# Last batch of expert units: the second-layer weights by plain SyncE transfers, the second bias by VectorE, and another order at the hand-over

## The reference, cut to what matters

```python
idx = jnp.argmax(probs, axis=-1)
pos = (jnp.cumsum(one_hot, axis=0) * one_hot).sum(-1).astype(jnp.int32) - 1
kept = pos < C
buf = jnp.zeros((E, C, D), dtype=h.dtype).at[idx, pos_safe].set(x, mode='drop')
hmid = jax.nn.relu(jnp.einsum('ecd,edf->ecf', buf, w1) + b1[:, None, :])
ybuf = jnp.einsum('ecf,efd->ecd', hmid, w2) + b2[:, None, :]
y_tok = ybuf[idx, pos_g] * (prb * kept)[:, None]
```

## Time and profile before

| | |
|---|---|
| median of 3 runs | 2496.98 us (2493.55 to 2497.48) |
| profiled execution, its own time | 2497.35 us |
| its span, first to last instruction | 2495.6 us |
| PE / DVE / ACT / POOL busy | 82% / 61% / 41% / 74% |
| mean granted TensorE clock | 0.930 of full speed |
| PE busy from 2320 to 2340 us | 20.00 of 20 us |
| second-bias products L1279 | 105, 22 of them in the last batch |

### The profile page before, as it was taken

The page is one execution under the profiler, slowest core; times in us unless marked ns, Lnnn a source line. Parts: engine busy times, 40 slices in busy tenths (PEclk is TensorE's granted clock), DMA queues, the critical chain, the costliest instruction groups (busy, mean ns, idle before and its releaser), DMA issues. The chain is left out here.

```text
span 2495.6 us, 42607 instructions
## 1 busy us (share of the span) xinstructions
PE 2049.6 (82%) x12873; PEld 1578.1 (63%) x12873; DVE 1511.6 (61%) x5293; ACT 1033.6 (41%) x2479; POOL 1849.9 (74%) x1924
## 2 busy tenths in 40 slices
PE   0048999994677787998989989998989998787997
PEld 0015666662455565776768777776778777676986
DVE  6776555554358777787747556566565666565332
ACT  4663333331244444543434433443444444352332
POOL 7777777777777777777777777777777777765575
PEclk9999999996788887999999999999998999898999
DMA  9846666664566667777777777777887888778653
GB/s 337 321 138 178 174 175 175 175 172 128 150 195 201 194 190 255 237 238 222 244 232 227 248 231 234 233 229 253 304 295 273 306 304 293 249 274 305 239 180 108
DMA packets 279195, 568.84 MB, mean 228 GB/s; under 512 B 51493, under 2 KB 180142, under 8 KB 259791
## 3 DMA queue, kind: packets, MB, share of 16 engines
q0 software_dynamic: 98352, 268.90, 35.3%
q1 hardware_dynamic: 150225, 245.97, 28.9%
q10 hardware_dynamic: 30390, 51.21, 5.6%
HBM read 506.09 MB, written 87.86 MB: 238 GB/s over the span
## 5 line engine op out<-in xcount | busy, mean ns | idle before, releaser
L967 POOL DMA_INDIRECT rows_sb<-xn_scratch,src_sb x1517 | 1458.3, 961 | 462.2 <-issue 456.7
L1261 PE MATMUL bank<-acc 128*128 128x128 f32 (+1 forms) x2624 | 434.4, 319 | 3.6 <-ACT acc L2042 2.9
L1285 PE MATMUL bank<-acc 128*128 128x256 f32 x1680 | 413.1, 390 | 0.0
L1261 PEld LDWEIGHTS bank<-acc 128*128 128x128 f32 x2624 | 379.2, 202 | 27.3 <-issue 5.6
L1079 PE MATMUL bank<-rows_sb,s_sb 128*24 128x256 f32 x3082 | 229.7, 419 | 198.6 <-DMA rows_sb<-xn_scratch,src_sb 198.0
L2059 ACT ACTIVATE acc<-bank,acc 128x128 f32<-128x128 f32 (+1 forms) x656 | 211.9, 398 | 368.5 <-PE bank L1261 368.2
L1285 PEld LDWEIGHTS bank<-acc 128*128 128x128 f32 x1680 | 313.9, 194 | 48.8 <-issue 0.4
L1549 DVE TENSOR_TENSOR acc<-acc,bank 128x48 f32 x831 | 170.5, 205 | 264.8 <-PE bank L1089 150.2
L1079 PEld LDWEIGHTS bank<-rows_sb,s_sb 128*24 128x24 f32 x3082 | 85.5, 108 | 272.8 <-issue 240.4
L1976 ACT COPY sums<-bank 120x256 f32<-120x256 f32 x208 | 76.5, 368 | 355.6 <-PE bank L1079 355.5
L2007 ACT ACT_TABLE_LOAD x95 | 121.9, 1283 | 200.8 <-PE bank L1168 199.9
(11 more groups left out here) (277 smaller groups left out, 3633.7 us busy)
## 6 DMA issues: line engine op xcount, KB each, us to landing
acc<-ffn_first_in SPq DMA_DIRECT2D x64, 1028.0 KB
acc<-ffn_w_in SPq DMA_DIRECT2D x64, 1024.0 KB
arena<-xn_scratch SPq DMA_DIRECT2D x194, 128.0 KB, 3.1
h_scratch<-arena ACTq DMA_DIRECT2D x97, 256.0 KB
rows_sb<-xn_scratch,src_sb POOLq DMA_INDIRECT x1517
xnt_scratch<-arena SPq DMA_DIRECT2D x97, 128.0 KB, 2.3
arena<-xnt_scratch SPq DMA_DIRECT2D x97, 128.0 KB
arena<-x_in SPq DMA_DIRECT2D x97, 128.0 KB
```

The lines of the kernel that those rows point to most:

```text
L967: pool.indirect_dma_start(out=chunk_row(c), out_offset=None, in_=xn_d, in_offset=bass.IndirectOffsetOnAxis(ap=src_sb[:, c:c + 1], axis=0)) ...
L1261: m = pe.matmul(bank[:, i * tokens:(i + 1) * tokens], w1_sb[k % 2][:, h, f * P:(f + 1) * P], xt[:, k % 2, h, 0:tokens], start=h == 0, stop ...
L1285: m = pe.matmul(bank[:, i * D:(i + 1) * D], hid[:, f, i * P:(i + 1) * P], w2_sb[k % 2][:, f, :], start=False, stop=f == FC - 1 and i == 0)
```

## The change

- GpSimd's `load_new_second` goes. SyncE loads the second-layer weights of all 22 units of the last batch in full, whether the expert is a new one or not. The first-layer loads stay as they are.
- For the last batch TensorE's bias product, its mask and the wait for it go. SyncE loads the unit's bias row to all partitions (`load_bias`, 128 KB), behind the second-layer loads of a place, and VectorE's `finish_unit` does one operation more, (bias x probability) + y.
- The last batch's order changes. `wanted_at` is one place later, so that unit 60's tokens are turned at the head of tick (60, 1), place 220, and no longer in tick (59, 2), place 219; by the planner's arithmetic no other tick, gather or load moves. At place 216 TensorE does the `sums` products before the two ticks (58, 1) and (58, 2), which stood on either side of them. VectorE reads `sums` at once, queues the units after four of the seven tables, and does the unit finishes of places 215 to 217 (units 56 and 57) only after the slots are filled. Their scatters move to place 218, behind the gathers of units 60 and 61.

```diff
+        b2_sb = [rows_sb[:, ROW_SLOTS - 2 + i, :] for i in range(2)]
...
+        HELD = range(chosen_at[-1], last_c + 1)
...
-        wanted_at = [slots_at[b] + (4 if slots_at[b] + 4 < PAIRS else 2) for b in batch_of]
+        wanted_at = [slots_at[b] + (4 if slots_at[b] + 4 < PAIRS else 2 if slots_at[b] < PAIRS else 3) for b in batch_of]
...
-            if e_place[n] == sums_at[-1] and ("unit", n - 1) not in here:
-                here.insert(0, ("unit", n))
-            elif e_place[n] >= PAIRS or ("unit", n - 1) in here or after == len(here):
+            if e_place[n] >= PAIRS or ("unit", n - 1) in here or after == len(here):
                 here.append(("unit", n))
...
+            if k in FINAL:
+                b2_at[max([known] + [done_place(k - 2) + 1] * (k - 2 in FINAL))].append(k)
...
-            scatter_at[min(done_place(k) + 1, PLACES - 1)].append(k)
+            scatter_at[last_c + 1 if done_place(k) in HELD else min(done_place(k) + 1, PLACES - 1)].append(k)
...
+            def load_bias(k):
+                x_ = expert_of(k)
+                sp.wait_ge(pair_mm, PAIRS)
+                if k - 2 in FINAL:
+                    sp.wait_ge(y_done, k - 1)
+                sp.dma_start(b2_sb[k % 2], ffn_b2[bass.ds(x_, 1), :].broadcast_to([P, D])
+                             ).then_inc(b2_ld[k % 2], 16)
...
                 for k in w2_at[p]:
-                    if k not in SKIPS:
-                        load_second(k)
+                    load_second(k)
                 for k in keep_at[p]:
                     keep_unit(k)
+                for k in b2_at[p]:
+                    load_bias(k)
...
-                for k in w2_at[p]:
-                    if k in SKIPS:
-                        load_new_second(k)
...
-                    if k in SKIPS:
-                        pe.wait_ge(new2_ld[k % 2], new_value(k))
-                    else:
-                        pe.wait_ge(w2_ld[k % 2], w2_value(k))
-                    pe.wait_ge(hot_spread, k + 1)
+                    pe.wait_ge(w2_ld[k % 2], w2_value(k))
+                    if k not in FINAL:
+                        pe.wait_ge(hot_spread, k + 1)
...
-                    for i, col in enumerate(columns_of(k)):
+                    for i in range(size(k) if k not in FINAL else 0):
                         pe.matmul(bank[:, i * D:(i + 1) * D], hot_wide.bitcast(F32R), b2_parts.bitcast(F32R),
                                   start=i == 0, stop=False)
...
+                    if k == sums_at[-1]:
+                        for n, at in enumerate(e_place):
+                            if at == k:
+                                unit_tick(n)
                     read_small(k, False)
                 elif kind == "end":
-                    read_small(k, True)
+                    if k != rank_at[-1]:
+                        read_small(k, True)
...
                             build_table(t)
+                            if t == routes[-1][RT - 1]:
+                                read_small(k, True)
...
-                if k < K and j == 1:
+                if k < FINAL[0] and j == 1:
...
+                    if k in FINAL:
+                        dve.wait_ge(b2_ld[k % 2], b2_value(k))
+                        link(dve.scalar_tensor_tensor(y[:, 0, :], b2_sb[k % 2], sprb[:, columns_of(k)[0]:columns_of(k)[0] + 1],
+                                                      y[:, 0, :], ALU.mult, ALU.add))
...
-                for kind, k in side[p]:
-                    if kind == "unit" and p >= PAIRS:
-                        finish_unit(k)
+                if p >= PAIRS and p not in HELD or p == last_c:
+                    for n, at in enumerate(e_place):
+                        if at == p or p == last_c and at in HELD:
+                            finish_unit(n)
```

More of the change, by code:

```diff
@@ L314, in build @@
         zero_st, far_kept, acc_ld = sem("zero_st"), sem("far_kept"), sems("acc_ld", 4)
-        new1_ld, new2_ld, rows_known = sems("new_w1_ld", 2), sems("new_w2_ld", 2), sem("rows_known")
+        new1_ld, b2_ld, rows_known = sems("new_w1_ld", 2), sems("b2_ld", 2), sem("rows_known")
         dve_seq, act_seq = sem("dve_seq"), sem("act_seq")
@@ L554, in build @@
         sums_at = [p + 1 for p in chosen_at]
+        HELD = range(chosen_at[-1], last_c + 1)
+        assert HELD[0] > PAIRS and rank_at[-1] == sums_at[-1] == build_at[-1]
         def most_ticks(p):
@@ L607, in done_place @@
             return e_place[last_tick[k] + FLUSH]
-        w1_at, w2_at, gather_at, scatter_at = ([[] for _ in range(PLACES)] for _ in range(4))
+        w1_at, w2_at, b2_at, gather_at, scatter_at = ([[] for _ in range(PLACES)] for _ in range(5))
+        assert all(size(k) == 1 for k in FINAL)
         for k in range(K):
@@ L614, in build @@
             w2_at[max([known] + [place_of(k - 1, 2)] * (k > 1))].append(k)
+            if k in FINAL:
+                b2_at[max([known] + [done_place(k - 2) + 1] * (k - 2 in FINAL))].append(k)
             lag = wanted_at[k] - slots_at[batch_of[k]] - 1
             ahead = 1 if turn_place[k] < PAIRS + 2 else 3
-            asked = max(known - 1 + lag, turn_place[k] - ahead)
+            asked = max(known - 1 + lag if slots_at[batch_of[k]] < PAIRS else known, turn_place[k] - ahead)
             if wanted_at[k] >= PAIRS:
@@ L652, in new_value, with b2_value @@
             return 16 * ((k - SKIPS[0]) // 2 + 1)
+        def b2_value(k):
+            return 16 * ((k - FINAL[0]) // 2 + 1)
         def w2_value(k):
@@ L1020, in load_new_first @@
                     bounds_check=NE * P - 1, oob_is_err=False).then_inc(new1_ld[k % 2], 16)
[L1022 to L1028, removed]
             for p in range(PLACES):
@@ L1285, in second_layer @@
                         m = pe.matmul(bank[:, i * D:(i + 1) * D], hid[:, f, i * P:(i + 1) * P], w2_sb[k % 2][:, f, :],
-                                      start=False, stop=f == FC - 1 and i == 0)
+                                      start=k in FINAL and f == 0 and i == 0, stop=f == FC - 1 and i == 0)
                 m.then_inc(l2_mm, 1)
@@ L1791, in side_step @@
                             build_table(t)
+                            if t == routes[-1][RT - 1]:
+                                read_small(k, True)
                 elif kind == "unit":
-                    unit_tick(k)
+                    if e_place[k] != sums_at[-1]:
+                        unit_tick(k)
                     if e_place[k] < PAIRS:
```

## The result

The changed kernel takes 2507.11 us (median of 6 runs, 2504.58 to 2511.04) against 2497.68 us (6 runs, 2493.55 to 2499.53): a ratio of 1.0034, 95% interval [1.0023, 1.0045]. It is 0.34% slower; the forecast was 2497.6 us, with a range to 2503.5. The profiled executions differ by 9.0 us in span (2504.6 against 2495.6).

The account below looks back on a forecast made before the run. The prediction took TensorE to bound the tail (busy 20.00 of 20 us). Its terms, -6.8 - 2.7 + 0.5 - 1.5 + 11.1, gave +0.6 us: 2497.6 us against the median, overall range 2487 to 2503.5.

Parts of the forecast that it names:

- SyncE's queue: Last batch: second-layer loads behind load-backs come late, stalling units 67 and 71 by 5.4 us each, unit 75 by 0.3: +11.1 us.
- T: The end of unit 65's first layer, from which the forecast counted load 67's times; units 71 and 75 are counted likewise.
- Unit 75: Its second-layer load stands behind load-back 9, of half the size, with no real first-layer load beside it: 0.3 us.
- Bias products: TensorE in the last batch: 22 products of 0.31 us leave the path, units 7.44 us apart: -6.8 us.
- GpSimd's loads: Tail: five issues a unit instead of six let GpSimd keep pace, so TensorE's stalls go: -2.7 us.
- The hand-over: Before unit 60: earlier table reading and new order gain, partly lost waiting for unit 59's mask: -1.5 us.
- VectorE's added operation: Counts only behind the last unit, between ScalarE's scaling and the last scatter: +0.5 us.
- Added traffic: Twelve formerly skipped 1.05 MB loads and 22 of 128 KB: nothing, up to +3 us in the first six units.
- The queue costs more: Rival: load 67 lands last, unit 75 loses 2 us too, 2503 us; chance 0.20, shared with an unseen added stall.

Follow-up runs that it names:

- the kernel with the order alone: The kernel before with only the new hand-over order, bias products and second-layer loads as before: 2496.39 us, ratio 0.9985 to the kernel before.
- the kernel with both mends: The changed kernel with weight loads ahead of the load-back in SyncE's queue and unit 59's mask ahead of units 56 and 57's finishes: 2486.43 us.
- the run without it: The changed kernel with the second-layer loads of units 64 to 81 given back to GpSimd: 2500.56 us, ratio 1.0000 to the kernel before.
- The run with the mask first: The changed kernel with VectorE writing unit 59's mask ahead of the finishes of units 56 and 57: 2506.06 us, ratio 1.0026 to the kernel before.
- the kernel with all mends: The changed kernel with weight loads before load-backs, unit 59's mask before the finishes, same-expert second-layer loads skipped, and small load-backs whose buffers are already free: 2478.89 us.
- the kernel with the loads first: The changed kernel with weight loads ahead of the load-back within each place of SyncE's queue: 2489.76 us, ratio 0.9962 to the kernel before.

## Why the prediction was wrong

Step by step, by its own terms; sizes are those of the profiled execution.

- **SyncE's queue, forecast +11.1 us: this is the step that failed.** Place, order and releaser were right: load-back 7 goes out at T + 8.84 us (forecast T + 8.65; T is 2346.50), load 67 at T + 10.03 (T + 9.75), and TensorE waits, then works at the low clock. The size was wrong, in three parts. Load 67 landed at T + 20.4 instead of T + 19.1, past even the upper end of T + 20.1, and was needed at T + 14.7; the wait is 5.71 us and not 4.2, unit 71's 4.90. The low clock costs 2.2 to 2.8 us behind each wait and not 1.2: eight products take 3.54 instead of 1.73 us, and the next group is 0.4 us or more longer. And unit 75, put at 0.3 us because its load-back is half as large and no real first-layer load goes out beside it (which is so: that of 2431.78 landed in 2.2 us), has the longest wait, 6.97 us. The three cost 17.6 + 7.3 = 24.9 us, above this term's upper end of 14, so the range fell short.
- **Unit 75.** The error was to count bytes and leave the wait out. Load-back 9 went out at 2432.93, T + 12.4 us with T at 2420.51, 3.6 us later than load-backs 7 and 8 (both T + 8.84), and load 75 right behind it. It was in use 8.1 us after its issue, so that with no such delay the wait would still have been some 3.4 us by my estimate (6.97 - 3.58), and not 0.3. Of the 3.6 us 2.3 arise at GpSimd's first-layer load of that place (T + 4.57 instead of T + 2.24), as its timeline shows:

```profile
2420.97 0.98 POOL L1014 DMA_INDIRECT out_dram<-acc,sca_i  x1 [0.30 <-issue]
2425.08 1.05 POOL L1033 DMA_INDIRECT acc<-ffn_first_in,acc  x1 [3.12 <-ACT acc L2075]
```

- **Bias products, forecast -6.8 us.** Right in sign and too small: the interval between units fell by 0.50 us (7.75 to 7.25: 2308.73 to 2315.97 us for units 60 and 61) and not 0.31, 10.8 us in all. The distance from the product's start to the next group's holds only part of its price; the groups around it are longer too: the first-layer group ahead of a second layer takes 1.79 us from start to start here (2306.94 to 2308.73) and 1.88 in the kernel with the order alone, which has the bias product behind it, and the second-layer group 1.73 (2308.73 to 2310.46) and 1.83: 0.31 + 0.09 + 0.10 = 0.50.
- **GpSimd's loads, forecast -2.7 us.** The stalls of GpSimd's own making went, but short waits for first-layer weights (2.6 us) took their place, which shrink when SyncE's loads are halved (8.3 to 2.7 us, on the kernel with both mends). Zero in sum. The other half of its value was missed: in the run without it the bias shows no gain.
- **The hand-over, forecast -1.5 us.** Right: -2.2 us, by the forecast mechanism. (The forecast's own pieces, 2304.4 + 0.4 + 0.6, give 2305.4 and not 2305.9, so -2.0.) The mask comes 20.1 us after unit 58's load (forecast 21.2), TensorE idles 3.73 us (3.5), the second layer takes 3.57 us (3.5). The run with the mask first shows the wait to be that of the two finishes.
- **VectorE's added operation, forecast +0.5 us.** Right: the last scatter is issued 8.11 us after unit 81's first second-layer group (2489.31 to 2497.42), against 7.69 before (2478.82 to 2486.51).
- **Added traffic, forecast 0.** In the first six units there was one wait of 1.3 us, for unit 64's first-layer load. Later it is not nothing: loads 67, 71 and 75 themselves are part of it, none of which has to move anything.

With the measured sizes the sum is -2.2 for the hand-over, -10.8 for the bias (21 x 0.5 + 0.3), 28.3 - 2.7 = +25.6 for all that is lost in the tail, and +0.4 for VectorE: +13.0 us. The first mark came 2.1 us sooner in this execution and the last transfer landed 1.9 us sooner after its issue, which leaves the 9.0 us between the spans; the medians differ by 9.4. Of the rivals "The queue costs more" came closest; its threshold, stalls over 15.5 us, was passed by far.

The prediction drew on the Trainium skill (DMA: Bandwidth & Descriptors, Queues, rings and completion order) for load 67 ending about with load 68 of the first layer. The trace agrees: load 68, issued at 2356.00 us, landed 11.0 us later, at 2367.0; TensorE took load 67 at 2366.87. What was too small was the time that both need: load 68 of the first layer landed in 7.1 us before and in 11.0 here, where load 67 and load 68 of the second layer (2359.32) went out beside it.

Left open: how much of the 21 us is the wait and how much the size of the load-backs, since small ones were never put into the changed kernel with the wait kept. Also why GpSimd held its issue back until 2425.08 us although the relu it waited for had ended at about 2421.9, 3.2 us earlier, where 0.9 us is usual. The DMA engines were over 90% busy in those microseconds, which is no proof. And the four waits of the first layer in the kernel that skips loads were read from its trace and not tested alone, beyond their shrinking in the kernel with all mends.

## What to carry to other kernels

A queue that only issues transfers is an engine like any other: before a load is moved to it, ask what it may be blocked on when the buffer of that load comes free. Here turning the order around in a queue that blocks gave back 17 us, and four small buffers that never block gave back 21, with the same bytes. And ask first whether the load has to move anything: the three that came late did not.

Two edits that relieve different engines of one loop are priced together. Shorter products showed no gain with GpSimd at 8.0 us a unit, and 0.5 us a unit once it was under that.

Price a stall as idle time plus what follows it at the lower clock, here 17.6 and 7.3 us, and don't take a burst's price from bytes over mean bandwidth.

## What the runs showed of the hardware

- After waits of 4.9 to 7.0 us TensorE's granted clock was 0.50 and eight 128x256 products took 3.54 us instead of 1.73; after a wait of 1.3 us they took no longer. In the kernel with the loads first 1.7 us were lost behind a wait of 3.0 us (granted 0.71, then 0.50), and 0.1 us behind one of 2.0 us (granted 1.00).
- TensorE started on a 1 MB load that went out behind a 1 MB load-back, beside two more of 1 MB, 10.3 us after its issue, on another like it after 9.5 us, and on the one behind a 0.5 MB load-back after 8.1 us.
- A bias product of 16 rows by 256 columns cost 0.50 us of the interval between units, where its start-to-start distance shows 0.31.
- GpSimd's indirect load at 2425.08 us started 3.2 us after the end of the relu that the profile names as its releaser, where 0.9 us is usual.
